# Attention stage of a fused two-layer kernel: scores two units ahead, scaling one ahead, both heads' values in one product 256 wide, keys turned per unit in one bank, expert choice in three parts

## What is computed

```python
scores = jnp.einsum('bghtd,bgsd->bghts', qg, k_all) * SCALE
allowed = (kpos[None, None, :] <= pos[:, :, None]) & (kpos[None, None, :] > pos[:, :, None] - WINDOW)
scores = jnp.where(allowed[:, None, None, :, :], scores, -jnp.inf)
p = jax.nn.softmax(scores, axis=-1)
o = jnp.einsum('bghts,bgsd->bghtd', p, v_all).reshape(Bx, H, Tx, HD)
...
return jnp.einsum('bto,do->btd', o, Wo)
...
logits = jnp.clip(xt @ gate_w.T, -50.0, 50.0)
top_w, top_idx = jax.lax.top_k(logits, TOP_K)
rw = jax.nn.softmax(top_w, axis=-1)
```

## Time and profile before

| | us |
|---|---|
| median of 3 runs (1231.78 to 1240.38) | 1237.12 |
| the profiled execution's own time | 1237.26 |
| its span in the profile | 1235.7 |
| busy: PE | 1050.6 (85%) |
| busy: DVE | 673.4 (54%) |
| busy: ACT | 379.8 (31%) |
| busy: POOL | 436.7 (35%) |

### The profile page before, as it was taken

The page is one execution under the profiler, slowest core; times in us unless marked ns, Lnnn a source line. Parts: engine busy times, 40 slices in busy tenths (PEclk is TensorE's granted clock), DMA queues, the critical chain, the costliest instruction groups (busy, mean ns, idle before and its releaser), DMA issues.

```text
span 1235.7 us, 15748 instructions
## 1 busy us (share of the span) xinstructions
PE 1050.6 (85%) x4469; PEld 712.5 (58%) x4469; DVE 673.4 (54%) x1892; ACT 379.8 (31%) x820; POOL 436.7 (35%) x500
## 2 busy tenths in 40 slices
PE   4899999999999906788988888888898885996995
PEld 4787577578478405455555555555555553775774
DVE  5655897787797773744344444444433434342332
ACT  3422422322332623733333333333332321111110
POOL 3213344444300534232233433333333402454452
PEclk7699999999999955677666677777766667998998
DMA  8364421321400524312111121112121102562451
GB/s 240 135 242 150 188 76 27 94 57 9 125 35 1 188 78 135 112 56 60 54 50 52 52 60 56 57 47 60 56 59 47 50 1 67 146 185 81 138 186 37
DMA packets 66362, 109.67 MB, mean 89 GB/s; under 512 B 29811, under 2 KB 31107, under 8 KB 66158
## 3 DMA queue, kind: packets, MB, share of 16 engines
...
q10 hardware_dynamic: 944, 1.74, 0.5%
...
## 4 chain that ended last, share of the span: by engine, by line
PE 40%; DVE 8%; DMA 5%; issue 4%; ACT 3%; POOL 1%; POOLq 0%; DVEq 0%; SPq 0%
PE bank L1616 11%; PE bank L1631 8%; PE bank L1605 6%; DMA y_in<-yx_dram,mine 4%; PE bank L1720 4%; PE bank L1574 3%; PE bank L1625 2%; DVE prob L1860 2%; PE bank L1596 1%; DVE kT_lo L1828 1%; DVE experts_lo L1919 1%; PE bank L1710 1%; PE bank L1582 1%; ACT pT L1760 1%; ACT oT L1770 1%
## 5 line engine op out<-in xcount | busy, mean ns | idle before, releaser
L1616 PE MATMUL bank<-pT,kv_t 128*64 128x128 f32 (+1 forms) x768 | 171.1, 363 | 0.0
L549 POOL DMA_INDIRECT kv_t<-in_kv_cache,own_cache x64 | 65.6, 1025 | 233.5 <-PE bank L1616 220.4
L1605 PE MATMUL bank<-ident,prob 128*128 128x128 f32 (+1 forms) x384 | 87.6, 359 | 70.7 <-DVE prob L1860 67.5
L1616 PEld LDWEIGHTS bank<-pT,kv_t 128*64 128x64 f32 (+1 forms) x768 | 102.3, 173 | 66.9 <-issue 56.9
L557 POOL DMA_INDIRECT kv_t<-kv_dram,own_new x96 | 97.8, 1018 | 102.5 <-DMA kv_t<-in_kv_cache,own_cache 66.3
L1853 DVE CUSTOM_DVE_ANT_0 prob<-bank,mask 128x320 f32<-128x320 f32 x128 | 60.6, 483 | 107.1 <-PE bank L1596 101.6
L730 PE MATMUL bank<-wqkv,x1T 128*128 128x512 f32 x256 | 112.1, 593 | 1.3 <-ACT x1T L836 1.3
L1605 PEld LDWEIGHTS bank<-ident,prob 128*128 128x128 f32 (+1 forms) x384 | 47.4, 160 | 103.6 <-DVE prob L1860 92.0
L1631 PE MATMUL bank<-wo,oT 128*128 128x512 f32 x128 | 102.9, 979 | 0.0
L1760 ACT ACTIVATE pT<-bank 128x384 f32<-128x384 f32 x128 | 61.3, 494 | 123.8 <-PE bank L1605 83.8
L730 PEld LDWEIGHTS bank<-wqkv,x1T 128*128 128x128 f32 x256 | 47.7, 190 | 57.4 <-issue 57.4
...
## 6 DMA issues: line engine op xcount, KB each, us to landing
...
```

The costliest lines, as they stand in the source:

```text
L549: pool.indirect_dma_start(kv_t[q % KVB][:, c, :], None, kv_cache, bass.IndirectOffsetOnAxis(own_cache[:, at:at + 1], 0), bounds_check=POOL ...
L1605: mm = pe.transpose(bk(2 + s % 2)[0:rows, c * P:(c + 1) * P], prob[:, s % PROBS, c * P:c * P + rows], ident[:, :])
L1616: mm = pe.matmul(bk(4)[g * HD:(g + 1) * HD, (2 * b + gp) * P:(2 * b + gp + 1) * P], kv_t[(2 * p + b) % KVB][0:rows, c, v:v + HD], pT[0:row ...
```

## The change

- `score` is issued two units ahead of `turn_p` instead of one, and `normalize` one unit ahead: in iteration `n`, PE issues `score(n+2)`, `turn_p` of unit `n`, `turn_k(n+3)`, `values(n-1)`; DVE issues both `masked` of unit `n+2`, both `normalize` of unit `n+1`, `kT_copy(n+3)`; ACT issues both `exponential` of unit `n+1`, both `pT_copy` of unit `n`, `kT_copy(n+3)`. The buffers `prob` grow from 4 to 6.
- `turn_k` works per unit (3 transposes) in bank 5 alone, with a ring of 3 buffers for the keys. Bank 7 becomes a second bank for the values' products, so that `oT_copy` runs per sequence, in two copies of 64 partitions. `places` and `logits` write into bank 5.
- `values` multiplies both halves in one product: 3 products of 128 columns of weights with 256 moving columns, of whose results half is used.
- `project_o`, with `places` and `logits`, moves from the end of iteration `at == 1` to that of `at == 2`, `turn_q` from `at == 2` to `at == 1`.
- The mask is made by one instruction; the scale of it goes into the scores' scale and `masked`.
- The choice of experts is cut: `rank` at the end of `at == 3`, `choose` at the end of `at == 0`, `weigh` at the end of `at == 1`, `place_entry` at the head of `at == 3`.
- POOL issues the third newly written piece (`gather_own`, 64 rows) ahead of its wait for the cache's rows.

```diff
...
-        kT_hi = place("kT_hi", (P, 2, 2, KEYS), F32R)
+        KRING = 3
+        kT_hi = place("kT_hi", (P, KRING, KEYS), F32R)
+        prob_5 = place("prob_5", (P, KEYS))
...
+        kT_lo = place("kT_lo", (P, KRING, KEYS), F32R)
+        prob = [place(f"prob{r}", (P, KEYS)) for r in range(5)] + [prob_5]
+        PROBS = len(prob)
+        pT = place("pT", (P, 2, NCH, 2, P))
...
+        def gather_own(pool, q):
+
+            c, rows = NCH - 1, KCH[NCH - 1]
+            at = q * NCH + c
+            pool.indirect_dma_start(kv_t[q % KVB][0:rows, c, :], None, kv_dram, bass.IndirectOffsetOnAxis(own_new[0:rows, at:at + 1], 0),
+                                    bounds_check=TOK - 1, oob_is_err=False).then_inc(kv_gathered[q % KVB], 16)
+
...
-            for c, rows in enumerate(KCH):
+            for c, rows in enumerate(KCH[:NCH - 1]):
...
-        K_BANKS = (5, 7)
-        UNITS = 4 * PAIRS
+        O_BANKS = (4, 7)
+        UNITS = 2 * B
...
-                    pool.wait_ge(kv_gathered[q % KVB], q // KVB * GATHERS + 16 * 2)
...
+                def turn_k(n):
+
+                    q, gp = n // 2, n % 2
+                    if gp == 0:
+                        pe.wait_ge(kv_gathered[q % KVB], (q // KVB + 1) * GATHERS)
+                    if n >= 1:
+                        pe.wait_ge(kT_ready, n)
+                    for c, rows in enumerate(KCH):
+                        mm = pe.transpose(bk(5)[:, c * P:c * P + rows], kv_t[q % KVB][0:rows, c, gp * P:(gp + 1) * P], ident[0:rows, 0:rows])
...
+                def values(n):
+
+                    q, gp = n // 2, n % 2
+                    pe.wait_ge(pT_ready, 2 * n + 2)
+                    if gp == 0 and q >= 2:
+                        pe.wait_ge(oT_ready, q - 1)
+                    v = (G + 2 * gp) * HD
                     for c, rows in enumerate(KCH):
-                        mm = pe.matmul(bk(4)[g * HD:(g + 1) * HD, (2 * b + gp) * P:(2 * b + gp + 1) * P], kv_t[(2 * p + b) % KVB][0:rows, c, v:v + HD],
-                                       pT[0:rows, s % TURNED, c, :], start=(c == 0), stop=(c == NCH - 1))
-                    if s % 4 == 3:
+                        mm = pe.matmul(bk(O_BANKS[q % 2])[:, gp * 2 * P:(gp + 1) * 2 * P], kv_t[q % KVB][0:rows, c, v:v + 2 * HD],
+                                       pT[0:rows, n % 2, c, :, :].rearrange("p g t -> p (g t)"), start=(c == 0), stop=(c == NCH - 1))
+                    if gp == 1:
                         mm.then_inc(o_ps, 1)
...
+                for n in range(2):
+                    turn_k(n)
+                    score(n)
+                turn_k(2)
...
-                    p, at, more = n // 4, n % 4, n // 4 + 1 < PAIRS
-                    if at == 2 and more:
-                        pe.wait_ge(kT_ready, p * 4 + 4)
-                        if p >= 1:
-                            pe.wait_ge(lg_read, p)
-                        turn_k(p + 1, 0)
-                    if at == 3 and more:
-                        pe.wait_ge(kT_ready, p * 4 + 6)
-                        turn_k(p + 1, 1)
-                    if n + 1 < UNITS:
-                        score(n + 1)
-                    if at == 2 and more:
-                        if p >= 1:
-                            pe.wait_ge(y_ready, p)
+                    p, at = n // 4, n % 4
+                    if n + 2 < UNITS:
+                        score(n + 2)
+                    if at == 1 and p + 1 < PAIRS:
+                        if p >= 2:
+                            pe.wait_ge(y_ready, p - 1)
                         turn_q(p + 1)
                     turn_p(2 * n)
                     turn_p(2 * n + 1)
+                    if n + 3 < UNITS:
+                        if at == 3 and p >= 1:
+                            pe.wait_ge(lg_read, p)
+                        turn_k(n + 3)
                     if n >= 1:
-                        values(2 * n - 2)
-                        values(2 * n - 1)
-                    if at == 1 and p >= 1:
-                        pe.wait_ge(kT_ready, p * 4 + 4)
+                        values(n - 1)
+                    if at == 2 and p >= 1:
+                        pe.wait_ge(kT_ready, min(n + 4, UNITS))
                         if p >= 2:
                             places(p - 2)
                         logits(p - 1)
+                        if p + 1 < PAIRS:
+                            pe.wait_ge(qT_ready, 2 * p + 4)
                         project_o(p - 1)
 
                 final = PAIRS - 1
-                values(8 * PAIRS - 2)
-                values(8 * PAIRS - 1)
+                values(UNITS - 1)
...
-                def kT_copy(p, b):
-                    act.wait_ge(kT_ps, p * 2 + b + 1)
-                    for gp in range(2):
-                        act.activation(kT_hi[:, b, gp, :], bk(K_BANKS[gp])[:, 0:KEYS], ACT.Copy).then_inc(kT_hi_ready, 1)
+                def kT_copy(n):
+                    act.wait_ge(kT_ps, n + 1)
+                    act.activation(kT_hi[:, n % KRING, :], bk(5)[:, 0:KEYS], ACT.Copy).then_inc(kT_hi_ready, 1)
...
+                def oT_copy(q):
+                    act.wait_ge(o_ps, q + 1)
+                    if q >= 2:
+                        act.wait_ge(y_ps, q // 2)
+                    for g in range(2):
+                        rows = slice(g * HD, (g + 1) * HD)
+                        o = act.activation(oT[rows, :, q % 2, :].rearrange("p (a h) t -> p a h t", a=2),
+                                           bk(O_BANKS[q % 2])[rows, :].rearrange("p (a g h t) -> p a g h t", a=2, g=2, h=2)[:, :, g, :, :], ACT.Copy)
+                    o.then_inc(oT_ready, 1)
...
-                    p, at, more = n // 4, n % 4, n // 4 + 1 < PAIRS
-                    exponential(2 * n)
-                    exponential(2 * n + 1)
+                    p, at = n // 4, n % 4
+                    if n + 1 < UNITS:
+                        exponential(2 * n + 2)
+                        exponential(2 * n + 3)
+                    if at == 1:
+                        if p + 1 < PAIRS:
+                            qT_copy(p + 1)
+                        if p >= 1:
+                            oT_copy(2 * p - 1)
+                    pT_copy(2 * n)
+                    pT_copy(2 * n + 1)
+                    if n + 3 < UNITS:
+                        kT_copy(n + 3)
                     if at == 0 and p >= 2:
                         route_exp(p - 2)
-                    if at == 2:
+                    if at == 3:
+                        oT_copy(2 * p)
                         if p >= 1:
                             y_copy(p - 1)
-                        if more:
-                            kT_copy(p + 1, 0)
-                            qT_copy(p + 1)
-                    pT_copy(2 * n)
-                    pT_copy(2 * n + 1)
-                    if at == 0 and p >= 1:
-                        oT_copy(p - 1)
-                    if at == 3 and more:
-                        kT_copy(p + 1, 1)
...
+                def make_mask(q):
+
+                    dve.scalar_tensor_tensor(out=mask[:, q % 2, :], in0=jrow[:, :], scalar=thr[:, q:q + 1], in1=band[:, :],
+                                             op0=ALU.is_lt, op1=ALU.max).then_inc(mask_ready, 1)
...
+                    dve.tensor_scalar(lg[:, :], bk(5)[:, 0:E], 50.0, -50.0, ALU.min, ALU.max).then_inc(lg_read, 1)
+
+                def rank(p):
...
+
+                def choose(p):
...
                 for n in range(UNITS):
-                    p, at, more = n // 4, n % 4, n // 4 + 1 < PAIRS
-                    if at == 2:
-                        normalize(2 * n)
-                        normalize(2 * n + 1)
-                        masked(2 * n + 2)
-                        masked(2 * n + 3)
-                    else:
-                        for s in (2 * n, 2 * n + 1):
-                            normalize(s)
-                            if n + 1 < UNITS:
-                                masked(s + 2)
-                    if at == 0 and p >= 2:
-                        weigh(p - 2)
-                    if at == 1:
+                    p, at = n // 4, n % 4
+                    if at == 3 and p >= 1:
                         if p >= 2:
                             place_entry(p - 2)
-                        if p >= 1:
-                            read_logits(p - 1)
-                        if more:
-                            make_mask(p + 1, 0)
-                    if at == 2 and more:
-                        kT_copy(p + 1, 0)
+                        read_logits(p - 1)
+                    if n + 2 < UNITS:
+                        masked(2 * n + 4)
+                        masked(2 * n + 5)
+                    if n + 1 < UNITS:
+                        normalize(2 * n + 2)
+                        normalize(2 * n + 3)
+                    if at == 1 and p + 1 < PAIRS:
                         qT_copy(p + 1)
-                    if at == 3:
-                        if more:
-                            make_mask(p + 1, 1)
```

(13 more changed lines are left out.)

122 lines of the change are left out of this document (49 added, 73 removed).

## The result

The changed kernel takes 1033.91 us (median of 4 runs, 1029.77 to 1037.33); beside it the kernel before took 1234.45. The ratio is 0.8371, 95% interval 0.8321 to 0.842: faster by 16%. The profiled execution took 1034.5 with a span of 1032.8, to be held against 1235.7 before.

What follows compares the result with a forecast made beforehand. PE was taken to bound the attention, through its half-speed clock and a 2.12 us wait for scaled rows. Fourteen pairs going from 34.13 to 20.8 us take 187 off 1237.3, giving 1050, range 1025 to 1135.

Steps and rivals of the forecast that it cites:

- That the clock holds: PE's clock: one rise in the first `project_o`, then 1.00; pair 19.3 to 23 us, total 1030 to 1081; chance 0.64.
- six units' worth of work: PE in the kernel before: the wait for scaled rows costs 2 us and the clock for six units' work.
- The unit: PE's work per unit at full speed: 3.37 us, of which values 1.45, between 1.2 and 1.88.
- The loop through DVE: From scores to keys' low part: 3.4 us with hand-overs at 3 and 0, 4.9 at 1.
- The iteration at 2: PE: unit 3.4, `places` and `logits` 1.3, `project_o` 3.6; together 8.3 us.
- The pair: Four iterations sum to 20.0 us; 0.2 four times for hand-overs makes 20.8, if the clock holds.
- The ends: First pairs lose some 5 us, the last pair gives about as much back; taken as zero.
- POOL (0.13): POOL or the gathers bound while the clock holds: a pair of 24 us, 1096 in total; chance 0.13.
- The fall once a pair (0.16): Third case: the clock falls at `at == 1`; pair 30.3 us, total 1184; chance 0.16.
- The two cases with the clock down behind `project_o` (0.04, 0.03): All four units at half speed: pair 36.9, total 1276, chance 0.04; one at full speed: 33.6, no change, 0.03.
- The rule on transposes: PE's clock: transposes do not bring the full clock; they are 1.22 of a unit's 3.37 us.
- the third and the fourth: Clock falls once a pair: 1184 us, chance 0.16; clock falls right behind `project_o`: 1276 us, chance 0.04.

Runs made afterwards that it cites:

- dve_late: The changed kernel with six extra DVE reductions over 320 columns behind `choose`; 1095.9 us, ratio 0.8837.
- before_choice_parts: The kernel before with only the choice of experts cut into parts on DVE; 1184.5 us, ratio 0.9574.
- choice_whole: The changed kernel with `rank` and `choose` together at the end of the iteration at 3, `weigh` at the end of that at 0; 1044.9 us.
- choose_later: The changed kernel with `choose` behind the iteration at 1 and `project_o` ahead of `places` and `logits`; 1030.8 us.
- own_behind: The changed kernel with the third, 64-row transfer again behind POOL's wait for the cache's rows; 1031.4 us.
- choose_later_q: Also called the last run: the changed kernel with `choose` and `project_o` moved as in `choose_later`, and the queries' load ahead of the result's store; 1026.2 us.

## Why the prediction was right, and where it was off

**That the clock holds** was right, and its reason was right in the main: the wait of 2.1 for scaled rows is gone, and what is left of waits brings the clock down at most now and then. `dve_late` puts a long wait back and gets the falls back. But the reason was told too simply. The prediction laid the fall to the one long wait; `before_choice_parts` has no wait over 1.42 in its pairs, and the clock falls in every one of them. So that the change would take away enough of the waits was in part luck. The rise that lasted came earlier than forecast, at 527.5 and not in the first `project_o`, behind four short ones. What was said to remain, a wait of about 1.1 at `at == 1`, is there for DVE's part (0.4 to 0.9). The queries' load, which waits in the same iteration, was not named; it brought the wait of 2.09 and the one fall.

One reading of the rows was wrong: at half speed there ran not six units' worth of work but the rest of one unit, one whole unit, `places`, `logits` and most of `project_o`. The 20.5 us were read rightly, and nothing in the sum rested on the six.

**The unit** was sized within 0.1: 3.30 for 3.37, the values 1.42 for 1.45. The 1.45 was a choice between 1.2 and 1.88, nearer to the row of long products; that direction had a reason, that it hit within 0.03 is luck.

**The loop through DVE** was right in both places: 3.44 at 0 for 3.4 (DVE comes to the scores 1.1 after their start, just behind `rank`), 4.82 at 1 for 4.9, with the parts that the sum named, the mask and `choose`. `choice_whole` and `choose_later` move these parts, and the time goes with them. ACT's end of 4.0 in that iteration was right too (3.87 in the last run), and is the next bound.

**The iteration at 2**: 8.52 for 8.3, of which `places` and `logits` 1.36 for 1.3, `project_o` 3.61 for 3.6, and the unit 3.54 for 3.4.

**The pair**: 20.08 undisturbed, for 20.0; between the first copies the mean is 20.60 (539.1 to 806.9, 13 pairs), for 20.8. The 0.2 for each hand-over didn't come as such. In its place stand, on average over the pairs, the waits for the queries' load and for late gathers, which the prediction had at nothing: it moved `turn_q` an iteration ahead and `project_o` an iteration back in its account of PE, and did not follow SyncE's queue, where the load for the one stands behind the store of the other. The sum came out right by two errors that met, which is luck.

**The ends** are the step that failed, and most of the 16 us. The prediction took zero: 5 lost at the first pairs, 5 given back at the last. At the start nothing was lost: the first copy came at 539.1, where it had been at 540.5. The prediction had the first `project_o` at half speed; the clock was at 1.00 from 527.5 on, and it took 3.61 like the later ones. At the end, the last two copies came after 15.83 and 7.41, where the sum had 20.8 and, with the ends taken at nothing, 15.2 as before. `project_o` an iteration later in its pair leaves an iteration less behind it in the last one, and the last pair makes no keys, queries or scores for a next. The whole error is 16.3: 2.6 from the pairs (13 x 0.2), 5.0 and 7.8 (15.2 - 7.4) from the last two copies, 1.4 ahead of the first copy, less 0.5 behind the last.

**The rivals.** POOL (0.13): not so. It takes 18.2 of 20.1 us a pair with its waits for landings, inside the 17.0 to 19.6 forecast, and `own_behind` costs nothing. Single gathers are late even so, by 0.35 and 0.90; once `choose_later_q` has brought the pair to 19.6, three are, by 0.3 to 0.95. The fall once a pair (0.16) did not come; `dve_late` makes it real, at the place and from the cause that were named. Its price, 30.3, was too high: the prediction let the clock stay down from the wait through `project_o` in every pair, and in `dve_late` it is back after 3 to 7 us in half of them, and in the other half inside `project_o`, with a pair of 27.1. The two cases with the clock down behind `project_o` (0.04, 0.03) did not come.

**The rule on transposes** that spoke against this (the Trainium skill, TensorE: Matmul & The Clock Gate, Part 4: PE-mode transpose) is contradicted by the changed kernel's trace further than the prediction went. The clock does not only keep 1.00 over units of which 1.23 of 3.30 are transposes. From 586.07, when it was at 0.50, to 589, when it was at 1.00, PE ran transposes and nothing else: those of queries, rows and keys, in the rows above. The clock had been at 1.00 up to 585.5, so this shows a return after a short fall; no run here shows a first rise over transposes alone. Neither of the two cases that the prediction named with the rule, the third and the fourth, came.

**Where the 200 us come from**, by the runs. The parts don't add: taken back one at a time from the changed kernel, they cost 24 (look-ahead), 13 (wide values), 11 (choice in parts) and nothing (POOL), 48 together; put one at a time into the kernel before, two of them give 52 each and 80 together. What makes the difference is whether the clock falls and stays down in each pair. Of the parts that were taken back alone, none is needed for it to hold; of those put into the kernel before, neither alone nor both together are enough.
